# A recurrent attention block on one core: staged operands spread out, value-key products moved to GpSimd, per-array transfer waits, and Ln with Exp for the roots

## The chip, the cores and the metric

The kernel runs on one core of one Trainium2 chip. Its time is device microseconds of one launch; lower is better. Engine names: PE is TensorE, DVE is VectorE, ACT is ScalarE, POOL is GpSimd, SP is SyncE (it only issues transfers here). PSUM is the accumulator memory that PE writes, SBUF the on-chip memory of all engines.

## What is computed

The whole kernel is four pairs of a mixing layer and a feed-forward or expert layer on a tensor `x` of 16 x 256 x 128. The change lies in the first block only, a recurrent attention ("rwkv") with 16 heads of 8 channels and its feed-forward part. Cut to what matters:

```python
def _wkv7(r, w_log, k, v, a, b):
    decay = jnp.exp(-jnp.exp(w_log))
    def step(state, inp):                     # state: batch, head, 8 x 8
        r_t, d_t, k_t, v_t, a_t, b_t = inp
        sa = jnp.einsum('bhij,bhj->bhi', state, a_t)
        state = state * d_t[:, :, None, :] + sa[..., None] * b_t[:, :, None, :] \
                + v_t[..., None] * k_t[:, :, None, :]
        return (state, jnp.einsum('bhij,bhj->bhi', state, r_t))
    ...
kk = kk / jnp.maximum(jnp.linalg.norm(kk, axis=-1, keepdims=True), 1e-12)
o = _wkv7(rh, w_log..., kh, vh, -kk, kk * ah)
o = _gn_heads(o.reshape(Bx, Tx, C), gn_w, gn_b)      # a norm per head, eps 0.00064
x = x + (o + bonus) * g @ W_o
x = x + jnp.square(jax.nn.relu(kf @ W_ffn1)) @ W_ffn2
```

## The kernel before, in words

The block is `rwkv_block` (line 2446). It runs three stages, each a block of its own with a barrier behind it.

**Arrays** (`rwkv_arrays`, line 2481). It loops over 8 pairs of sequences, 512 positions each, in tiles of 128 x 512. PE makes nine products per pair (`items`), with `LENGTHS`, the cross products (`cross`) and the late ones (`late`) between them; ACT takes them out of PSUM (`take`); DVE mixes (`blend`), and does the elementwise work of the pair before (`products`, `across`, `finish`) and of this one (`key`), and the norms of the next (`normalise`, `turn_rows`). `pad` on ACT writes the transposed rows that the next `blend` waits for. Two time steps are folded into one, so the scan has 128 steps. The results sit in the buffers `sent[s]` (r, w, k, v, b), `decay_two[s]` and `keep[s]`, two of each. SP sends them when a pair is finished, with twelve transfers into the scan's layout (five arrays of 2 x 128 KB, decays 2 x 64 KB; line 2547) and one of 768 KB to memory (`kept`, line 2550). ACT, before it takes item `k` of pair i, waits for all of pair i - 2 (lines 2641 and 2642). The lengths of the keys are rooted by ACT (Sqrt, line 2663), clamped and inverted by DVE (lines 2717, 2721). The loops of ACT and DVE are written as loops over pairs of pairs.

**Scan** (`rwkv_scan`, line 2813). 128 steps in 16 blocks of `CK` = 8. The state of a step is 128 partitions x 128 elements (two heads a partition, 8 x 8 each). ACT's `stage(m)` copies a block's operands out of the time-strided arrays (lines 2852 to 2858) into two slots. Per step, DVE multiplies the state in PSUM with the recall and decay vectors (`recalled`, line 2954, two instructions of 192 elements, the vector repeated over i by its access pattern), sums over j (`sa`, line 2960), makes `removed` (line 2964, one instruction of 256 elements for both folded steps), `shown` (line 2974, two instructions of 128) and the next step's value-key products `added` (line 2941). PE adds up the new state in the other PSUM bank: two matmuls with the identity for `added`, one for the decayed state, two for `removed` (lines 2911 to 2917), and in between one eighth of the output sums of the block before (`turn_out`, line 2899).

**Output** (`rwkv_out`, line 2997). Per pair of sequences: the mean and variance per head, the root (Sqrt on ACT, line 3099, reciprocal on DVE, line 3164), the gate, the output product, and the feed-forward part with four hidden tiles. ACT takes the hidden tiles out with Relu (line 3113), POOL squares them (line 3134). ACT does the root of pair i + 1 ahead of `padded` of pair i (`square(i + 1)`, then `ffn.act`), which DVE's `mix` (line 3200) and then PE's hidden matmuls (line 3077) wait for.

Each engine runs its own list in order; semaphores are the only link between them.

## Time and profile before

| what | us |
|---|---|
| median of three runs | 5173.32 (5163.14 to 5174.13) |
| profiled execution, its own time | 5184.22 |
| its span | 5182.1 |
| PE busy in the span | 3937.7 (76%) |
| DVE busy | 2686.7 (52%) |
| ACT busy | 2047.1 (40%) |
| POOL busy | 1004.0 (19%) |

The profile is of one execution. Busy time is that of instructions with work; waits and the issue of transfers don't count. Each part of the block has its own limit, so the shares of the whole span say little about it; the stretches and the timeline do. In a timeline row stand the start, the time, the engine, the line and the operation, output and inputs, and the number of instructions merged.

### The profile page before, as it was taken

The page shows a single profiled execution, that of the slowest core. Times are in us where ns is not written, and L with a number is a line of the kernel's source. Part 1 is how long each engine was busy: PE and PEld are TensorE (multiplying, and loading weights), DVE is VectorE, ACT ScalarE, POOL GpSimd, SP SyncE. Part 2 cuts the span into 40 slices and gives each one's busy share as a digit, 9 for nine tenths or more (in the row PEclk, how much of TensorE's full clock was granted, in tenths as well). Part 3 has the DMA queues.
Part 4 walks back from the last instruction along what each step waited for, and adds up shares of the span by engine and source line. Part 5 has one row for each costly group of instructions (what it writes and reads, how often), then busy time and mean ns, then how long its engine had stood idle before and what let it go on. Part 6 is the DMA issues. An engine that isn't in the chain of part 4 may idle for free. (4 is left out here: it accounts for less than half of the span.)

```text
span 5182.1 us, 64858 instructions
## 1 busy us (share of the span) xinstructions
PE 3937.7 (76%) x19738; PEld 2738.9 (53%) x19800; DVE 2686.7 (52%) x6897; ACT 2047.1 (40%) x4136; POOL 1004.0 (19%) x970
## 2 busy tenths in 40 slices
PE   3548976699976688868886988897899877720498
PEld 1116644377753365646664766675577655520266
DVE  5758967322224676657774344333222255579444
ACT  3322111244433288858883344333333333300132
POOL 1000003100000376546651000000000001144200
PEclk9769987799987699989997999998999966655599
DMA  1440011000000000000000000000000000000000
GB/s 28 64 67 6 4 57 36 37 1 0 0 4 16 17 1 0 1 18 1 0 1 15 1 0 0 0 0 9 25 0 0 5 0 0 0 1 0 17 0 16
DMA packets 45619, 58.53 MB, mean 11 GB/s; under 512 B 14058, under 2 KB 37836, under 8 KB 44588
## 3 DMA queue, kind: packets, MB, share of 16 engines
q1 hardware_dynamic: 45484, 56.92, 4.7%
q8 instruction: 61, 1.00, 0.1%
q14 instruction: 74, 0.61, 0.0%
HBM read 34.87 MB, written 10.51 MB: 9 GB/s over the span
## 5 line engine op out<-in xcount | busy, mean ns | idle before, releaser
L418 PEld LDWEIGHTS bank<-moe_w,moe_hidden 128*128 128x128 f32 x5376 | 626.6, 192 | 78.5 <-issue 76.5
L418 PE MATMUL bank<-moe_w,moe_hidden 128*128 128x128 f32 x5376 | 630.3, 275 | 0.0
L408 PE MATMUL bank<-normed_t,moe_w 128*128 (+1 forms) x1344 | 615.8, 600 | 11.7 <-ACT moe_hidden L470 8.4
L546 DVE SCALAR_TENSOR_TENSOR branch<-bank,moe_weights,branch 128x128 f32<-128x128 f32 x768 | 216.4, 344 | 708.1 <-PE bank L418 704.0
L470 ACT ACTIVATE moe_hidden<-bank,moe_b 128x512 f32<-128x512 f32 x544 | 373.0, 687 | 505.5 <-PE bank L408 504.0
L90 POOL TENSOR_TENSOR branch_norm_shifted<-branch_norm_moments,eps 128x4 f32<-128x4 f32 x64 | 12.8, 200 | 1903.8 <-DVE branch_norm_moments L83 1903.8
L408 PEld LDWEIGHTS bank<-normed_t,moe_w 128*128 128x128 f32 x1344 | 245.0, 193 | 256.6 <-issue 240.4
L1465 DVE TENSOR_TENSOR ssm_mixer<-ssm_decay,bank 128x384 f32<-128x384 f32 x256 | 141.9, 554 | 301.0 <-PE bank L1151 263.3
L1960 POOL TENSOR_TENSOR local_size<-local_size,local_half_powers 128x8 f32<-128x8 f32 x128 | 257.2, 2009 | 201.5 <-DVE local_size L2026 197.5
L1281 ACT ACTIVATE ssm_decay<-bank 128x384 f32<-128x384 f32 x256 | 124.9, 491 | 327.3 <-PE bank L1132 327.2
L1664 PE MATMUL bank<-local_wqkv,local_shifted 128*128 128x512 f32 x384 | 209.5, 637 | 56.0 <-DVEq L2018 24.4
L843 PE MATMUL bank<-ident,attn_scaled 128*128 128x128 f32 x32 | 8.9, 435 | 249.6 <-DVE attn_scaled L808 249.6
L1848 ACT ACTIVATE local_probs<-bank,local_peak 128x128 f32<-128x128 f32 x512 | 182.1, 379 | 8.9 <-issue 8.4
L1067 PE MATMUL bank<-ssm_in_rows,ssm_wbc 128*128 128x512 f32 x256 | 142.6, 676 | 45.1 <-ACTq L1264 44.9
L1164 PE MATMUL bank<-ssm_mixer,ssm_x_wide 128*128 128x256 f32 x512 | 158.9, 392 | 19.4 <-DVE ssm_mixer L1465 19.4
L1150 PE MATMUL bank<-ssm_c_rows,ssm_b_rows 128*128 128x256 f32 x512 | 173.1, 421 | 0.0
L1952 POOL TENSOR_TENSOR local_turned_part<-local_raw,local_tables 128x512 f32<-128x512 f32 x128 | 165.8, 1295 | 28.1 <-ACT local_raw L1827 26.7
L1689 PE MATMUL bank<-local_k_t,local_q_t 128*128 128x128 f32 x1024 | 141.0, 283 | 23.5 <-ACT local_probs L1848 20.7
L1689 PEld LDWEIGHTS bank<-local_k_t,local_q_t 128*128 128x128 f32 x1024 | 140.4, 199 | 27.7 <-issue 20.4
L1965 POOL TENSOR_TENSOR local_probs<-local_probs,local_total 128x512 f32<-128x512 f32 x128 | 133.3, 1041 | 82.9 <-DVE local_total L2050 82.9
L2045 DVE TENSOR_REDUCE local_peak<-bank 128x4 f32<-128x512 f32 x128 | 88.4, 691 | 117.4 <-PE bank L1689 110.4
L843 PEld LDWEIGHTS bank<-ident,attn_scaled 128*128 128x128 f32 x32 | 5.7, 217 | 252.0 <-DVE attn_scaled L808 252.0
(532 smaller groups left out, 8966.8 us busy)
## 6 DMA issues: line engine op xcount, KB each, us to landing
rwkv_kept<-rwkv_keep SPq DMA_DIRECT2D x8, 768.0 KB, 18.5
moe_w<-in_moe_w_dram SPq DMA_DIRECT2D x2, 2304.0 KB
rwkv_gate<-rwkv_kept SPq DMA_DIRECT2D x8, 512.0 KB, 3.4
moe_w<-in_moe_w_dram SPq DMA_DIRECT2D x2, 2048.0 KB
rwkv_recv<-rwkv_sent_r SPq DMA_DIRECT2D x16, 128.0 KB
x<-rwkv_sent_w SPq DMA_DIRECT2D x16, 128.0 KB
rwkv_keys<-rwkv_sent_k SPq DMA_DIRECT2D x16, 128.0 KB
rwkv_values<-rwkv_sent_v SPq DMA_DIRECT2D x16, 128.0 KB
```

Of the source, the lines that this page charges most:

```text
L408: pe.matmul(hbank[n % 4][:], w1[:, e, f * P:(f + 1) * P], source_t[:, bass.ds(i * PN, PN)], start=True, stop=True).then_inc(hidden_up, 1)
L418: last = pe.matmul(obank[e % 2][:, t * P:(t + 1) * P], hid[:, e % 2, f, t * P:(t + 1) * P], w2[:, e, f, :], start=(f == 0), stop=(f == chu ...
L470: act.activation(hid[:, e % 2, f, :], hbank[n % 4][:], ACT.Gelu_apprx_tanh, bias=b1[:, n:n + 1] if bias else 0.0).then_inc(hidden_done, 1)
L546: last = dve.scalar_tensor_tensor(core.branch[:, t, :], obank[e % 2][:, t * P:(t + 1) * P], weights[:, i * PT + t, e - first_routed:e - fi ...
L1067: last = pe.matmul(bank[0:rows, :], wbc[:, n, :], source, start=True, stop=True)
L1150: pe.matmul(gb[:, 0:SEQ], b[:, s[0]:s[0] + P], c[:, s[0]:s[0] + SEQ], start=True, stop=True)
L1164: pe.matmul(ybank[:, c * SEQ:(c + 1) * SEQ], x[0], m[:, 0:SEQ], start=(k == 0), stop=False)
L1664: pe.matmul(bank[:], shifted[:, at, t * P:(t + 1) * P], wqkv[:, part * INNER:(part + 1) * INNER], start=True, stop=True).then_inc(a_up, 1)
L1689: last = pe.matmul(bank[:, w * P:(w + 1) * P], q_t[:, j, c, w, :], keys, start=False, stop=(w == WINDOWS - 1))
L1848: last = act.activation(probs[:, u % 2, w, :], sbank[u % 2][:, w * P:(w + 1) * P], ACT.Exp, bias=peak[:, u % 2, w:w + 1], accum_out=total[ ...
L1952: pool.tensor_tensor(turned_part[:, m % 2, :].rearrange("p (h s d) -> p h s d", s=2, d=HD // 2), rows, sines.broadcast_to([P, HEADS, 2, HD ...
L1960: pool.tensor_tensor(part, part, half_powers[:], ALU.pow).then_inc(scaled, 1)
```

## The change

In the arrays: each array has its own semaphores, and every engine waits for the array that it is about to write. Decays and rates are sent by SP after `products`, `recv` after `finish`, values, recall and keys by ACT (in the queue of ACT). The lengths are clamped by DVE out of PSUM at the end of a pair, and ACT makes the inverse root as exp(-0.5 ln). The loops over pairs of ACT and DVE are written out. In the scan: the staged vectors are written out over i by ACT, so `recalled` and `shown` are one instruction each; `added` is made by POOL; `removed` is made in two instructions with a signal each. In the output part: ACT makes the inverse root with Ln and Exp, and squares the hidden tiles.

```diff
+        def send(queue, n, i, buffer):
+            for j in range(2):
+                b = 2 * i + j
+                queue.dma_start(home[n][b * GROUPS:(b + 1) * GROUPS, :, :],
+                                buffer[:].rearrange("p (j t) -> p j t", j=2)[:, j, :]).then_inc(landed[n][i % 2], 16)
...
-                sp.wait_ge(arrays_ready, i + 1)
-                for array, buffer in zip(arrays, (*sent[s], decay_two[s])):
-                    for j in range(2):
-                        b = 2 * i + j
-                        sp.dma_start(array[b * GROUPS:(b + 1) * GROUPS, :, :],
-                                     buffer[:].rearrange("p (j t) -> p j t", j=2)[:, j, :]).then_inc(arrays_in, 16)
+                sp.wait_ge(rates_ready, i + 1)
+                send(sp, "d", i, decay_two[s])
+                send(sp, "b", i, sent[s][4])
+                sp.wait_ge(recv_ready, i + 1)
+                send(sp, "r", i, sent[s][0])
                 sp.wait_ge(keep_ready, i + 1)
-                sp.dma_start(kept[i], keep[s][:]).then_inc(kept_in, 16)
-            sp.wait_ge(kept_in, 16 * PAIRS)
-            sp.wait_ge(arrays_in, 16 * 12 * PAIRS)
+                sp.dma_start(kept[i], keep[s][:]).then_inc(kept_in[s], 16)
...
                 take("g2", keep[s][:, 1, :], ACT.Identity, g_ready)
-                if has_next:
+                act.wait_ge(values_ready, i + 1)
+                send(act, "v", i, v)
+                if i > 0:
+                    send_keys(i - 1)
+                if i < PAIRS - 1:
                     pad(i + 1)
-                act.wait_ge(lengths_up, i + 1)
-                act.activation(lengths[:], core.bank[LENGTHS][:], ACT.Sqrt).then_inc(lengths_ready, 1)
+                act.wait_ge(lengths_kept, i + 1)
+                act.activation(lengths[:], lengths[:], ACT.Ln)
+                act.drain()
+                act.activation(lengths[:], lengths[:], ACT.Exp, scale=-0.5).then_inc(lengths_ready, 1)
+            def send_keys(q):
+                act.wait_ge(keys_ready, q + 1)
+                send(act, "w", q, sent[q % 2][1])
+                send(act, "k", q, sent[q % 2][2])
...
-                dve.wait_ge(lengths_ready, q + 1)
-                dve.tensor_scalar(lengths[:], lengths[:], 1e-12, None, ALU.max)
                 dve.wait_ge(act_ready, q + 1)
                 dve.tensor_tensor(with_k, k[:], r[:], ALU.mult)
-                dve.drain()
-                dve.reciprocal(lengths[:], lengths[:])
                 dve.tensor_tensor(even(decayed_r), even(d[:]), even(r[:]), ALU.mult)
-                if reused:
-                    dve.wait_ge(arrays_in, (q - 1) * 16 * 12)
+                if q >= 2:
+                    dve.wait_ge(landed["d"][s], 32 * (q // 2))
                 dve.tensor_tensor(decay_two[s][:], even(d[:]), odd(d[:]), ALU.mult)
                 dve.drain()
+                dve.wait_ge(lengths_ready, q + 1)
                 dve.tensor_tensor(w[:], w[:], lengths[:], ALU.mult).then_inc(lengths_used, 1)
...
+            def keep_lengths(i):
+                dve.wait_ge(lengths_up, i + 1)
+                dve.tensor_scalar(lengths[:], core.bank[LENGTHS][:], 1e-24, None, ALU.max).then_inc(lengths_kept, 1)
...
-                    act.wait_ge(shown_ready, m - 1)
+                    act.wait_ge(shown_ready, (m - 1) * CK)
+                    act.wait_ge(added_ready, (m - 1) * CK)
...
-                act.activation(to_sa[:, slot, :, 0:2, :], by_step(recall_w), ACT.Identity)
-                act.activation(to_sa[:, slot, :, 2, :], decays[:, :, m * CK:(m + 1) * CK].rearrange("p x c -> p c x"),
-                               ACT.Identity)
+                def spread(out, array):
+                    for h in range(PH):
+                        act.activation(out[:, :, h * HD * HD:(h + 1) * HD * HD].rearrange("p c (i j) -> p c i j", j=HD),
+                                       array[:, h * HD:(h + 1) * HD, :].rearrange("p j c -> p c j").unsqueeze(2)
+                                       .broadcast_to([P, CK, HD, HD]), ACT.Identity)
+                steps = lambda array, s: array[:, :, at].rearrange("p x (c s) -> p x c s", s=2)[:, :, :, s]
+                for s in range(2):
+                    spread(to_sa[:, slot, :, s, :], steps(recall_w, s))
+                spread(to_sa[:, slot, :, 2, :], decays[:, :, m * CK:(m + 1) * CK])
+                for s in range(2):
+                    spread(to_out[:, slot, :, s, :], steps(recv, s))
                 act.activation(rows_of[:, slot, :, 0:2, :], by_step(rates), ACT.Identity)
                 act.activation(rows_of[:, slot, :, 2:4, :], by_step(keys), ACT.Identity)
-                act.activation(values_of[:, slot], by_step(values), ACT.Identity)
-                act.activation(to_out[:, slot], by_step(recv), ACT.Identity).then_inc(staged, 1)
+                act.activation(values_of[:, slot], by_step(values), ACT.Identity).then_inc(staged, 1)
...
+                    if not (isinstance(c, int) and c == 0):
+                        pe.wait_ge(shown_ready, c)
                     pe.matmul(bank, core.ident[:], added[:, s, 0, :], start=True, stop=False)
                     pe.matmul(bank, core.ident[:], added[:, s, 1, :], start=False, stop=False)
                     pe.wait_ge(recalled_ready, c + 1)
                     pe.matmul(bank, core.ident[:], recalled[:, s, 2, :], start=False, stop=False)
-                    pe.wait_ge(removed_ready, c + 1)
+                    pe.wait_ge(removed_ready, c * 2 + 1)
                     pe.matmul(bank, core.ident[:], removed[:, s, 0, :], start=False, stop=False)
+                    pe.wait_ge(removed_ready, c * 2 + 2)
                     pe.matmul(bank, core.ident[:], removed[:, s, 1, :], start=False, stop=True).then_inc(state_ready, 1)
...
+        @block.gpsimd
+        def _(pool):
+            def add(c, slot, k):
                 out = added[:, k % 2].rearrange("p s (x j) -> p (s x) j", j=HD)
                 v = values_of[:, slot, k].rearrange("p s x -> p (s x)").unsqueeze(2)
                 key = rows_of[:, slot, k, 2:4, :].rearrange("p s (h j) -> p (s h) j", j=HD).unsqueeze(2)
                 shape = [P, 2 * PH, HD, HD]
-                dve.tensor_tensor(out.rearrange("p (a i) j -> p a i j", i=HD),
-                                  v.rearrange("p (a i) o -> p a i o", i=HD).broadcast_to(shape),
-                                  key.broadcast_to(shape), ALU.mult).then_inc(added_ready, 1)
...
-                    for h in range(PH):
...
+                    dve.tensor_tensor(recalled[:, s], state.unsqueeze(1).broadcast_to([P, 3, ST]), to_sa[:, slot, k],
+                                      ALU.mult).then_inc(recalled_ready, 1)
                     dve.drain()
                     dve.tensor_reduce(sa[:].rearrange("p s x -> p (s x)"),
                                       recalled[:, s, 0:2, :].rearrange("p a (x j) -> p (a x) j", j=HD), AX.X, ALU.add)
                     dve.drain()
-                    shape = [P, 2 * PH, HD, HD]
...
+                    shape = [P, PH, HD, HD]
+                    for a in range(2):
+                        dve.tensor_tensor(
+                            removed[:, s, a].rearrange("p (h i j) -> p h i j", h=PH, j=HD),
+                            sa[:, a].rearrange("p (h i) -> p h i", i=HD).unsqueeze(3).broadcast_to(shape),
+                            rows_of[:, slot, k, a, :].rearrange("p (h j) -> p h j", j=HD).unsqueeze(2).broadcast_to(
+                                shape), ALU.mult).then_inc(removed_ready, 1)
                     if k == 0 and not (isinstance(m, int) and m < 2):
                         dve.wait_ge(summed, m - 1)
-                    for h in range(PH):
...
+                    now = dve.tensor_tensor(shown[:, slot, k], state.unsqueeze(1).broadcast_to([P, 2, ST]),
+                                            to_out[:, slot, k], ALU.mult)
+                    now.then_inc(shown_ready, 1)
...
-                act.activation(spread[:], core.bank[0][:], ACT.Sqrt, bias=cols[:, 4:5]).then_inc(rooted, 1)
+                act.activation(spread[:], core.bank[0][:], ACT.Ln, bias=cols[:, 4:5])
+                act.drain()
+                act.activation(spread[:], spread[:], ACT.Exp, scale=-0.5).then_inc(rooted, 1)
...
-                act.wait_ge(hidden_done, i * HC)
+                if has_tail:
+                    act.wait_ge(out_up, i)
                 for f in range(HC):
                     act.wait_ge(hidden_up, i * HC + f + 1)
                     act.activation(relu[:, f, :], core.bank[2 + f][:], ACT.Relu).then_inc(relu_done, 1)
+                    if f > 0:
+                        act.drain()
+                        act.activation(hidden[:, f - 1, :], relu[:, f - 1, :], ACT.Square).then_inc(hidden_done, 1)
+                act.drain()
+                act.activation(hidden[:, HC - 1, :], relu[:, HC - 1, :], ACT.Square).then_inc(hidden_done, 1)
...
-                pool.wait_ge(out_up, i)
-                for f in range(HC):
-                    pool.wait_ge(relu_done, i * HC + f + 1)
-                    pool.tensor_tensor(hidden[:, f, :], relu[:, f, :], relu[:, f, :], ALU.mult).then_inc(hidden_done, 1)
...
-                dve.reciprocal(spread[:], spread[:])
```

## Rows read from the trace of the kernel before

**Rows 1.** Busy time by stretch, the block's stages; stretch, length, engines, PE clock, DMA share, GB/s.
```profile
50.00:366.50 316.50, 155.87 (x272) 53.70 (x272) 225.97 (x513) 109.22 (x143) 19.33 (x32) 0.77 0.35 51
366.50:391.20 24.70, 0.00 (x0) 0.00 (x0) 0.04 (x1) 0.01 (x1) 0.00 (x0) 0.51 0.58 110
391.20:717.00 325.80, 302.67 (x1538) 210.97 (x1538) 281.49 (x897) 54.13 (x112) 0.00 (x0) 0.98 0.02 5
```

**Rows 2.** Busy time by stretch within the arrays; PE, PEld, DVE, ACT, POOL.
```profile
89.08:122.68 33.60, 18.77 (x34) 6.39 (x34) 28.17 (x65) 13.84 (x18) 2.42 (x4) 0.80 0.04 7
122.68:308.95 186.27, 95.70 (x170) 32.80 (x170) 140.83 (x320) 69.19 (x90) 12.08 (x20) 0.73 0.42 60
308.95:366.50 57.55, 27.54 (x40) 9.45 (x40) 38.21 (x67) 14.94 (x19) 0.00 (x0) 0.71 0.48 66
```

**Rows 3.** Waits of the arrays: who waited for whom, total, times, longest.
```profile
ACT rwkv_sent_w L2630 <- DMA rwkv_kept<-rwkv_keep: 75.7, 6, 13.4
```

**Rows 4.** Timeline at the end of a pair of the arrays.
```profile
118.17 0.60 ACT L2631 ACTIVATE rwkv_keep<-bank 128x512 f32<-128x512 f32 x1 [7.27 <-PE bank L2588]
...
120.32 1.26 SPq L2547 DMA_DIRECT2D x<-rwkv_sent_w  x2
...
121.83 0.78 ACT L594 ACTIVATE rwkv_padded<-bank,rwkv_cols 128x512 f32<-128x512 f32 x1 [3.06 <-PE bank L588]
```

**Rows 5.** Groups by line, arrays: busy us, mean ns, idle before.
```profile
L2721 DVE RECIPROCAL rwkv_squares<-rwkv_squares 128x512 f32<-128x512 f32 x8 | 26.8, 3353 | 0.6
```

**Rows 6.** Timeline of one step of the scan.
```profile
501.11 0.62 DVE L2954 TENSOR_TENSOR rwkv_recalled<-bank,rwkv_to_sa 128x192 f32<-128x192 f32 x2
...
502.32 0.43 DVE L2964 TENSOR_TENSOR rwkv_removed<-rwkv_sa,rwkv_rows_of 128x256 f32<-128x256 f32 x1
...
502.80 0.49 PE L2916 MATMUL bank<-rwkv_removed,ident 128*128 128x128 f32 x2
...
503.12 0.39 PE L2917 MATMUL bank<-rwkv_removed,ident 128*128 128x128 f32 x2
...
503.35 1.08 PE L2899 MATMUL bank<-rwkv_shown,ident 128*128 128x256 f32 x2
503.55 0.62 DVE L2954 TENSOR_TENSOR rwkv_recalled<-bank,rwkv_to_sa 128x192 f32<-128x192 f32 x2
...
504.71 0.39 PE L2914 MATMUL bank<-rwkv_recalled,ident 128*128 128x128 f32 x2
```

**Rows 7.** Groups by line, DVE products of other blocks with 384 and 128 elements.
```profile
L1465 DVE TENSOR_TENSOR ssm_mixer<-ssm_decay,bank 128x384 f32<-128x384 f32 x256 | 141.9, 554 | 301.0 <-PE bank L1151 263.3 <-ACT ssm_decay L1281 24.0 <-issue 12.9
...
L2010 DVE TENSOR_TENSOR local_tables<-local_tables,local_scales 128x128 f32<-128x128 f32 x4 | 0.9, 287 | 3.1 <-DMA local_masks<-in_window_dram 3.1
```

**Rows 8.** Groups by line, a POOL product of 256 elements.
```profile
L712 POOL TENSOR_TENSOR attn_products<-attn_qkv 128x256 f32<-128x256 f32 x3 | 2.4, 804 | 1.0 <-DVE attn_scores L753 1.0
```

**Rows 9.** Timeline of the local attention: a PSUM operand on DVE beside POOL.
```profile
2006.80 0.75 DVE L2085 SCALAR_TENSOR_TENSOR local_hidden<-bank,local_cols,local_bent 128x512 f32<-128x512 f32 x1
...
2006.89 1.04 POOL L1965 TENSOR_TENSOR local_probs<-local_probs,local_total 128x512 f32<-128x512 f32 x1 [1.48 <-DVE local_total L2050]
```

**Rows 10.** Timeline of one pair of the output part.
```profile
829.85 0.69 ACT L3099 ACTIVATE rwkv_spread<-bank,rwkv_out_cols 128x512 f32<-128x512 f32 x1 [2.16 <-PE bank L3050]
...
832.85 6.14 PE L3077 MATMUL bank<-rwkv_mix,rwkv_w 128*128 128x512 f32 x8 [3.04 <-DVE rwkv_mix L3200]
...
835.98 1.25 DVE L3166 SCALAR_TENSOR_TENSOR rwkv_centred<-rwkv_centred,rwkv_out_cols,rwkv_gate 128x512 f32<-128x512 f32 x1
...
842.89 1.92 PE L3064 MATMUL bank<-rwkv_wo,rwkv_gated 128*128 128x128 f32 x8
```

**Rows 11.** Groups by line, ACT's strided copies of the scan.
```profile
L2852 ACT ACTIVATE rwkv_to_sa<-x 128x256 f32<-128x256 f32 x16 | 10.1, 633 | 64.5 <-PEq L2487 46.9 <-DVE rwkv_shown L2974 17.5
...
L2853 ACT ACTIVATE rwkv_to_sa<-rwkv_decays 128x128 f32<-128x128 f32 x16 | 6.6, 415 | 0.0
```

**Rows 12.** Timeline of ACT in the wave block: the load ahead of an Exp that follows Ln.
```profile
1542.17 1.28 ACT L2226 ACT_TABLE_LOAD   x1
```

More of the change, by code:

```diff
@@ L2474, in rwkv_block, with rwkv_arrays @@
             decays = ssb("decays", [P, PC, STEPS])
-            rwkv_arrays(core, sem, heads, heads_in, arrays_in, kept_in, kept,
-                        (recv, recall_w, keys, values, rates, decays), GROUPS, HALF, DECAY)
+            rwkv_arrays(core, sem, heads, heads_in, kept, (recv, recall_w, keys, values, rates, decays), GROUPS, HALF,
+                        DECAY)
             rwkv_scan(core, sem, (recv, recall_w, keys, values, rates, decays), mixed_out, out_sent, x_back, x_dram)
         rwkv_out(core, tail, heads, kept, mixed_out, x_back)
-def rwkv_arrays(core, sem, heads, heads_in, arrays_in, kept_in, kept, arrays, GROUPS, HALF, DECAY):
+def rwkv_arrays(core, sem, heads, heads_in, kept, arrays, GROUPS, HALF, DECAY):
     nc, dram = core.nc, core.dram
@@ L2621, in pad, with pair @@
                 act.sem_inc(padded_ready, 1)
-            def pair(i, s, reused=True, has_next=True):
+            def pair(i):
+                s = i % 2
                 r, w, k, v, b = sent[s]
@@ L2940, in add_next, with steps, _ @@
                 shape = [P, 2 * PH, HD, HD]
-                dve.tensor_tensor(out.rearrange("p (a i) j -> p a i j", i=HD),
-                                  v.rearrange("p (a i) o -> p a i o", i=HD).broadcast_to(shape),
-                                  key.broadcast_to(shape), ALU.mult).then_inc(added_ready, 1)
-            def steps(m, slot, last=False):
+                if not (isinstance(c, int) and c < 2):
+                    pool.wait_ge(state_ready, c)
+                pool.tensor_tensor(out.rearrange("p (a i) j -> p a i j", i=HD),
+                                   v.rearrange("p (a i) o -> p a i o", i=HD).broadcast_to(shape),
+                                   key.broadcast_to(shape), ALU.mult).then_inc(added_ready, 1)
+            def steps(m, slot):
+                pool.wait_ge(staged, m + 1)
+                for k in range(CK):
+                    add(m * CK + k, slot, k)
+            steps(0, 0)
+            with pool.Fori(0, BLOCKS // 2 - 1) as h:
+                for slot in range(2):
+                    steps(h * 2 + 1 + slot, 1 - slot)
+            steps(BLOCKS - 1, 1)
+        @block.vector
+        def _(dve):
+            dve.memset(nothing[:], 0.0).then_inc(cleared, 1)
+            def steps(m, slot):
+                dve.wait_ge(staged, m + 1)
                 for k in range(CK):
@@ L2993, in _ @@
             steps(BLOCKS - 2, 0)
-            steps(BLOCKS - 1, 1, last=True)
+            steps(BLOCKS - 1, 1)
 def rwkv_out(core, tail, heads, kept, mixed_out, x_back):
```

119 lines of the change are left out of this document (49 added, 70 removed).

## The prediction

> **What bounds the kernel now.** I first cut the span into its stages with the table of stretches. The diff touches one block of nine, in three stages: the arrays (50 to 366.5 us), the scan (391.2 to 717) and the output part after it. Between the first two stand 24.7 us with no compute at all, while DMA is 58% busy [rows 1]. What follows the block isn't touched and is carried over.
>
> *Arrays.* VectorE (DVE) carries the pair. The pair from 89.08 took 33.60 us with DVE busy 28.17; the next five took 186.27, so 37.25 each, with the same DVE work (140.83 / 5 = 28.17) [rows 2]. The 3.65 us between them are waits, and the list of waits names their origin: ScalarE (ACT) stands 75.7 us in six waits, about 12.6 each, for the transfers of two pairs ago before it can take `k` [rows 3]. That holds up TensorE (PE), and through it DVE.
>
> *Scan.* The timeline shows a loop of dependences. `recalled` starts at 501.11, `removed` at 502.32, PE takes `removed` at 502.80, its second matmul at 503.12, and the next `recalled` starts at 503.55: 1.21 + 0.48 + 0.32 + 0.43 = 2.44 us [rows 6], and 128 of these are 312 of the 325.8 us [rows 1]. PE is nearly full beside it: from the second `removed` matmul (503.12) to `recalled` of the next step (504.71) is 1.59, plus 0.23 for that one (503.12 to 503.35 is the spacing of such a pair) makes 1.82, and 2.05 for the round [rows 6].
>
> **The change part by part.**
>
> *Arrays, middle.* (a) The DVE reciprocal goes, 3.35 us a pair [rows 5], and with it the maximum ahead of it, which moves to the end of the pair, where DVE waits for `padded` anyway; I count 3.6 for both. ACT gets Ln and Exp instead. They run while DVE mixes and does the first products of the next pair, so they cost nothing; if that cover went, it would be two table loads of 1.28 [rows 12] and two activations of about 0.6, 3.8 us a pair. (b) The waits for whole pairs become waits per array, on two queues. Decay and rates go right after `products`, values from ACT right after the g2 item, recall and keys before the next pad. The 12.6 us wait of ACT should go, and with it the 3.65 us on DVE. Bounds: 0 (all transfers as late as now) to 3.65; I take 3.65, because by the new order `w` is issued about 13 us ahead of the need for it (my estimate from the places of g2 and of the wait in the pair), behind four transfers of 128 KB, where now a whole pair's thirteen go out at once. (c) ACT now issues DMAs: six a pair stand between g2 and pad. SyncE pays 1.26 for two, so six cost 3.8 us. g2 starts at 118.17 and ends at about 118.8; pad could start at 122.6 instead of 121.83 [rows 4], so 0.8 to 0.9 later, and DVE's next mix waits for pad. Bounds 0 and 3.8. For pair 0 there are two sends: about +1.2. Sum: pair 0 +1.2; pair 1 -3.6 + 0.9 = -2.7; the five others -(3.6 + 3.65 - 0.9) = -6.35 each, -31.8.
>
> *Arrays, end.* The last stretch, 308.95 to 366.5, has DVE busy only 38.2 of 57.6 [rows 2]. ACT's wait there goes too (12.8 of it), but the last lengths now pass through six sends (3.8), a load, Ln, a load, Exp (3.8) before DVE may go on: I estimate -9, bounds -2 and -13. After it the 24.7 us: now the last pair's twelve sends and the 768 KB of `kept` all begin at its end. Afterwards only two sends of `recv` and `kept` begin there, with `w` and `k` 6 us earlier on their own queue. That leaves about half of the traffic: -11, bounds -4 and -17. Arrays together: 1.2 - 2.7 - 31.8 - 9 - 11 = -53.
>
> *Scan, the loop.* `recalled` becomes one instruction of 384 elements. The same kind with one operand in PSUM takes 554 ns [rows 7], now two take 0.62: -0.07. `removed` becomes two of 128 elements; such a one takes 287 ns [rows 7] against 0.43: the first matmul starts 0.14 earlier. The second half ends 0.2 later, and PE comes to it 0.32 after the first, so it isn't late. 2.44 - 0.21 = 2.23 a step; DVE itself needs less than 2 without `added`. 128 x 0.21 = -27; I take -26. Bounds: none, if PE's three more waits a step cost 0.2 us; -50, if the step falls to PE's 2.05.
>
> *Scan, GpSimd (POOL).* A product of 256 elements on POOL takes 804 ns in the attention block [rows 8]. It starts when the state of two steps ago is out, at the same moment as `recalled`, and is needed some 3 us later: hidden, twofold. Its price if it isn't lies in a rival.
>
> What it may disturb is DVE. The trace has both sides: a DVE instruction with one operand in PSUM took its usual 0.75 while POOL multiplied [rows 9], one with its tensors all in SBUF took 1.25 beside POOL [rows 10]. `recalled` and `shown` are of the first kind. `removed` is of the second, but starts 1.14 us after the state, when POOL's 0.80 are over. So zero.
>
> The Trainium skill ("SBUF — State Buffer", section "Who interferes with whom") says that a VectorE instruction with two SBUF inputs and a GpSimd one that reads SBUF exclude each other for the whole instruction. By that rule, the trace agrees for the SBUF case (1.25 against 0.75) and for the PSUM case; its own result is the third rival.
>
> *Scan, staging.* ACT now writes ten spread pieces of 512 elements instead of three smaller copies. The strided copies cost 415 ns for 128 elements and 633 for 256 [rows 11], 1.7 ns an element; 512 give 1.07, about 0.97 from start to start. Ten and the three others make 11.3 us a block against 3.1. Per block of eight steps (17.8 us) it fits and hides; at the start nothing hides it: +8. Bounds: +3 (if broadcast reads are as cheap as 256 elements now) and +12. Scan: -26 + 8 = -18.
>
> *Output part.* The reciprocal leaves DVE, the squares leave POOL (and DVE's 1.25 goes back to 0.75 [rows 9, 10]). But on ACT, Ln (0.69) is followed by a load of 1.28 and an Exp of 0.63 ahead of `padded`: Exp after Ln is loaded anew in the wave block [rows 12]. So `padded` and `mix` come 2.0 us later. The hidden matmuls start at 834.9 instead of 832.85, take 6.14, and with 0.7 for the transposes the next ones can start at 841.7 instead of 842.89 [rows 10]: -1 a pair, -7. Bounds: +2 a pair (+14) if ACT's squares hold PE, -3.4 a pair (-24).
>
> The skill's "ScalarE: Activation LUTs" (section "Table sets") says that one set holds both functions and Ln then Exp needs one load. The row of the wave block shows a load before each, so I go by the row; by the rule `padded` would be 1.3 us earlier and the part some 9 us shorter.
>
> **The sum.** -53 - 18 - 7 = -78. The profiled run took 5184.2, so 5106 for it. It stands 10.9 over the median of the three shown runs, 5173.3; against that median the forecast is 5095.
>
> **Rivals.**
>
> 1. *ACT as a DMA queue is in the way.* A send to a full queue stands still, and on ACT it holds pad and so DVE; and `w` may land late. For: six issues are 3.8 us of an in-order engine, and it is already 0.9 late by my sum. Against: at most six are outstanding. Price: 4 us a pair over seven pairs, 28. Total -50, 5123.
>
> 2. *PE is the bound of the scan.* For: 2.05 of 2.44 are matmuls, and three waits are added. Then the step stays near 2.4 and the scan gains 4 and loses 8 at the start. Total -53 + 4 - 7 = -56, 5117.
>
> 3. *The other side: POOL holds `removed`.* If POOL's product runs later than I think (it waits for its slot, or takes over 1.1 us), each step's two `removed` wait for it, up to its whole 0.80. The step is then 3.03, the scan +76 + 8, the total 84 - 53 - 7 = +24, 5197. It decides from 0.6 us a step on (the other terms give 52 us, or 0.41 a step, on top of the 0.21). For: all tensors of `removed` are in SBUF. Against: 0.34 us of distance.
>
> 4. *The staging on ACT doesn't fit a block.* It would take 1.55 us a piece; at 2 us a block is 22.0 against 8 x 2.44 = 19.5 now, and the scan +40: total -20, 5153.
>
> **How the numbers follow.** Forecast 0.60, rival 1 0.18, rival 2 0.11, rival 3 0.06, rival 4 0.03, and 0.02 for no change. A measurement of this kernel can tell about 0.2%, 10 us, from no change. Faster 0.89, same 0.04, slower 0.07. Low end: -53 - 11 more from the end of the arrays and the start, -26, -16 in the output part and the staging at +3, near 5060. High end: rivals 1 and 2 together with half of the bound in the output part, 5145.
>
> **What would show it.** Right: pairs of about 31 us in the arrays with no ACT wait of 12 us; a gap before the scan of 13 to 15 us; steps of 2.23; POOL near 0.8 busy per step and `removed` near 0.29; first `recalled` 11 us after the first staging piece; output pairs of 26. Wrong: `removed` above 0.4 (rival 3), PE without idle time in a step (2), pad waiting on ACT's own queue (1). The prediction falls if the transfers on two queues land no earlier than on one.

## The result, and the profile after

The changed kernel took 5095.72 us (median of four runs, 5086.59 to 5100.58) beside 5173.73 for the kernel before in the same comparison; the ratio is 0.9851, with a 95% interval of 0.9831 to 0.9871. The forecast was 5095. The time fits better than the parts do, so the parts are what is worth reading. The profiled execution took 5086.59 (span 5084.6) beside 5184.22: 97.6 less, against 78.0 between the medians; the forecast for it was 5106.

The milestones of both traces, in us:

| stretch | before | after | change | forecast |
|---|---|---|---|---|
| arrays, pair 0 (from 69.28 / 69.12) | 19.80 | 21.45 | +1.65 | +1.2 |
| arrays, pair 1 | 33.60 | 30.10 | -3.5 | -2.7 |
| arrays, five pairs | 186.27 | 152.91 | -33.4 | -31.8 |
| arrays, last stretch (to 366.5 / 320.5) | 57.55 | 46.92 | -10.6 | -9 |
| no compute, up to the scan | 24.7 | 10.4 | -14.3 | -11 |
| scan, start to first `recalled` | 3.1 | 11.0 | +7.9 | +8 |
| scan, first to last `recalled` | 311.4 | 285.9 | -25.5 | -26 |
| output, up to the first `delta` | 49.3 | 51.6 | +2.3 | 0 |
| output, seven pairs | 180.7 | 163.2 | -17.5 | -7 |
| output, last pair and up to the router | 41.7 | 41.8 | +0.1 | 0 |
| router of the first expert layer | 17.3 | 28.9 | +11.6 | 0 |
| all behind it | 4187.1 | 4171.0 | -16.1 | 0 |

These rows of stretches of the changed kernel answer to [rows 1, 2] and have their columns.

```profile
320.50:330.90 10.40, 0.00 (x0) 0.00 (x0) 0.00 (x0) 0.00 (x0) 0.00 (x0) 0.50 0.51 126
330.90:631.00 300.10, 285.51 (x1522) 206.07 (x1523) 231.40 (x641) 189.74 (x222) 80.28 (x128) 0.97 0.02 6
90.57:120.67 30.10, 18.60 (x34) 6.31 (x34) 25.20 (x64) 14.50 (x19) 2.41 (x4) 0.80 0.24 37
120.67:273.58 152.91, 89.81 (x170) 29.96 (x170) 125.65 (x316) 72.51 (x95) 12.07 (x20) 0.81 0.45 74
273.58:320.50 46.92, 23.96 (x40) 8.22 (x40) 31.49 (x64) 17.54 (x22) 0.00 (x0) 0.75 0.50 86
```

A pair of the arrays is 30.58 now (152.91 / 5), with DVE busy 25.13; before it was 37.25 with 28.17 busy. So 3.0 us of the 6.7 are work that left DVE, and 3.6 are waits that went. The transfers are spread over the whole pair (DMA 24% busy already in the second pair, where it was 4%), and ACT's wait of 12.6 us [rows 3] is gone. The end of one pair, from the timeline (start, length, engine, line, operation):

```profile
173.93 0.60 ACT L2644 ACTIVATE rwkv_keep<-bank 128x512 f32<-128x512 f32 x1 [3.23 <-PE bank L2600]
...
174.64 1.29 ACTq L2541 DMA_DIRECT2D rwkv_values<-rwkv_sent_v  x2
...
175.97 1.28 ACTq L2541 DMA_DIRECT2D x<-rwkv_sent_w  x2
...
177.28 2.07 ACTq L2541 DMA_DIRECT2D rwkv_keys<-rwkv_sent_k  x2
...
179.46 0.78 ACT L594 ACTIVATE rwkv_padded<-bank,rwkv_cols 128x512 f32<-128x512 f32 x1 [4.93 <-PE bank L588]
180.30 0.69 DVE L2731 TENSOR_TENSOR rwkv_delta<-rwkv_padded 128x512 f32<-128x512 f32 x1 [1.12 <-ACTq L2632]
```

ACT's six sends fill it from 174.64 to 179.35, and `pad` comes only then, DVE's `delta` behind it: this is what answers to [rows 4]. The six were costed at 3.8 us and take 4.2 to 5.3 in the seven pairs that have six: the last two (keys) take 1.5 to 2.6 instead of 1.26. The trace before has the same at the end of a pair, where the last two of twelve sends took 1.9 to 4.5.

One step of the scan, which answers to [rows 6]:

```profile
500.33 0.56 DVE L3010 TENSOR_TENSOR rwkv_recalled<-bank,rwkv_to_sa 128x384 f32<-128x384 f32 x1 [0.27 <-PE bank L2959]
500.37 0.63 POOL L2984 TENSOR_TENSOR rwkv_added<-rwkv_values_of,rwkv_rows_of 128x256 f32<-128x256 f32 x1 [1.61 <-PE bank L2959]
...
501.47 0.49 DVE L3018 TENSOR_TENSOR rwkv_removed<-rwkv_sa,rwkv_rows_of 128x128 f32<-128x128 f32 x2
501.49 0.39 PE L2955 MATMUL bank<-rwkv_recalled,ident 128*128 128x128 f32 x2
...
501.82 0.49 PE L2957 MATMUL bank<-rwkv_removed,ident 128*128 128x128 f32 x2
...
502.14 0.39 PE L2959 MATMUL bank<-rwkv_removed,ident 128*128 128x128 f32 x2
...
502.57 0.56 DVE L3010 TENSOR_TENSOR rwkv_recalled<-bank,rwkv_to_sa 128x384 f32<-128x384 f32 x1 [0.27 <-PE bank L2959]
```

1.14 + 0.35 + 0.32 + 0.43 = 2.24; the forecast was 2.23. POOL's product takes 0.63 and is over (501.00) 0.47 us before `removed` starts. Ahead of the steps stands the staging on ACT, thirteen pieces from 330.91 on, and the first `recalled` at 342.17.

One pair of the output part, which answers to [rows 10]:

```profile
769.50 1.28 ACT L3140 ACT_TABLE_LOAD   x1
...
770.80 0.69 ACT L3140 ACTIVATE rwkv_spread<-bank,rwkv_out_cols 128x512 f32<-128x512 f32 x1
...
771.54 1.28 ACT L3142 ACT_TABLE_LOAD   x1
...
772.83 0.63 ACT L3142 ACTIVATE rwkv_spread<-rwkv_spread 128x512 f32<-128x512 f32 x1
773.37 0.76 ACT L594 ACTIVATE rwkv_padded<-bank,rwkv_out_cols 128x512 f32<-128x512 f32 x1
774.20 0.69 DVE L3239 TENSOR_TENSOR rwkv_delta<-rwkv_padded 128x512 f32<-128x512 f32 x1 [1.93 <-ACTq L3150]
...
775.77 6.19 PE L3118 MATMUL bank<-rwkv_mix,rwkv_w 128*128 128x512 f32 x8 [5.11 <-DVE rwkv_mix L3243]
...
777.94 1.11 DVE L99 TENSOR_SCALAR fresh<-x,x_norm_moments,x_norm_rstd 128x128 f32 x4
...
781.79 0.60 PE L171 MATMUL bank<-ident,fresh 128*128 128x128 f32 x4
782.23 1.06 PE L3105 MATMUL bank<-rwkv_wo,rwkv_gated 128*128 128x128 f32 x8
```

A load stands before Ln and another before Exp, as forecast. From `mix` (774.96) to the next wo matmuls is 7.27 us; it was 10.85 (832.04 to 842.89, [rows 10]). DVE is done with `fresh` at 779.05, and PE comes to it only at 781.79, when the hidden matmuls (those of L3118) are through: PE sets that half of the pair now.

The router of the first expert layer, which the diff doesn't touch, before (first fence) and after (second), as rows of stretches (the first with PE alone, the second with all engines):

```profile
977.70:995.04 17.34, 16.93 (x81) 0.89 0.00 0
```

```profile
884.70:913.60 28.90, 28.50 (x81) 15.79 (x82) 1.79 (x16) 5.42 (x8) 0.00 (x0) 0.50 0.00 0
```

The same 81 matmuls ran at a mean granted clock of 0.89 before (0.50 for the first 3.5 us, then 1.00) and at 0.50, the lower level, throughout the 28.9 us after.

### The profile page after: what moved, and what is told of

Read it like the earlier page. It is cut to its first block and busy times, and to the rows that moved or that the text cites. A ratio compares the mean times of both kernels' runs of the same rounds, so it can differ in the third digit from the quotient of the medians.

```text
span 5084.6 us, 65295 instructions
## 1 busy us (share of the span) xinstructions
PE 3893.2 (77%) x19738; PEld 2713.3 (53%) x19800; DVE 2569.9 (51%) x6625; ACT 2231.9 (44%) x4312; POOL 1045.3 (21%) x1066
## 5 line engine op out<-in xcount | busy, mean ns | idle before, releaser
L470 ACT ACTIVATE moe_hidden<-bank 128x512 f32<-128x512 f32 x128 | 76.5, 597 | 152.1 <-PE bank L408 152.1
## 6 DMA issues: line engine op xcount, KB each, us to landing
rwkv_kept<-rwkv_keep SPq DMA_DIRECT2D x8, 768.0 KB, 15.2
```

What stands on the lines that cost most here:

```text
L470: act.activation(hid[:, e % 2, f, :], hbank[n % 4][:], ACT.Gelu_apprx_tanh, bias=b1[:, n:n + 1] if bias else 0.0).then_inc(hidden_done, 1)
```

## The experiments

The verdicts rest on stretches, each read from one trace, and not on the whole time, in which single runs of one kernel lie up to 0.5% apart. Where the code of a stretch is the same, it repeats: steps of the scan within 0.4% (2.246 to 2.254), pairs of the arrays 29.19 to 29.67 (nine traces), pairs of the output part 23.31 to 23.59 (nine). For the pairs and steps I give rows of tiles: least, middle and largest length in ns, and the first and last start; from these a pair is (last - first) / 7 and a step (last - first) / 127. The changed kernel's own rows are these (a pair of the arrays, a step, a pair of the output part), and the fourth is the output part before:

```profile
L2731 DVE TENSOR_TENSOR rwkv_delta<-rwkv_padded x8: 691/692/693, 69.1 to 273.6; 128x512 f32<-128x512 f32 x8
L3010 DVE TENSOR_TENSOR rwkv_recalled<-bank,rwkv_to_sa x128: 557/558/559, 342.2 to 628.1; 128x384 f32<-128x384 f32 x128
L3239 DVE TENSOR_TENSOR rwkv_delta<-rwkv_padded x8: 692/692/730, 679.7 to 842.9; 128x512 f32<-128x512 f32 x8
L3196 DVE TENSOR_TENSOR rwkv_delta<-rwkv_padded x8: 692/693/728, 755.3 to 936.0; 128x512 f32<-128x512 f32 x8
```

### The scan

**The products back on VectorE.**

```diff
-                pool.tensor_tensor(out...).then_inc(added_ready, 1)      # GpSimd
+                dve.tensor_tensor(out...).then_inc(added_ready, 1)       # VectorE, behind shown
```

> The changed kernel with one part undone: the value-key products go back from GpSimd to VectorE, behind `shown`. Two bounds theory (before, VectorE's own order and the loop of dependences both took 2.44 us, so each part of the scan's change pays only together with the other): VectorE's order is 0.65 + 0.49 + 0.41 + 0.34 + 0.48 = 2.37 us from start to start, the step is 2.37 in place of 2.24, and the scan is 16 us longer than in the changed kernel, the block too. Loop only (as the prediction told it): the step stays 2.24 and the time is the changed kernel's within noise.

```profile
L2993 DVE TENSOR_TENSOR rwkv_recalled<-bank,rwkv_to_sa x128: 552/558/559, 344.2 to 629.9; 128x384 f32<-128x384 f32 x128
```

The step is 2.25, as with GpSimd; the kernel took 5096.58 (a single run). My own favourite, two equal bounds with 2.37, falls. It had taken 0.48 for `added` from a step in which part of that was waiting; without a wait it is 0.35:

```profile
501.38 0.42 DVE L3008 TENSOR_TENSOR rwkv_shown<-bank,rwkv_to_out 128x256 f32<-128x256 f32 x1
...
501.71 0.41 DVE L2983 TENSOR_TENSOR rwkv_added<-rwkv_values_of,rwkv_rows_of 128x256 f32<-128x256 f32 x1
...
502.06 0.56 DVE L2993 TENSOR_TENSOR rwkv_recalled<-bank,rwkv_to_sa 128x384 f32<-128x384 f32 x1
```

VectorE is without a gap here, and the loop of dependences is just as long (2.24). The move to GpSimd earns nothing; it only leaves VectorE 0.27 us a step.

**Only that move.** Vectors staged compact, `recalled` and `shown` in two instructions, `removed` in one.

```diff
-                    dve.tensor_tensor(recalled[:, s], state..., to_sa[:, slot, k], ALU.mult)
+                    for h in range(PH):   # two of 192, vector repeated by its access pattern
+                        ...
```

> The changed kernel, but of the scan's changes only the move of the value-key products to GpSimd is kept: the vectors are staged compact again, `recalled` and `shown` are two instructions each, `removed` is one. Two bounds or loop only: the loop of dependences is that of before, so the step is 2.44 us, and VectorE stands idle some 0.4 us of it, waiting for TensorE; the scan loses 25 us in its steps against the changed kernel and gets 8 back at its start. Rival (before, the order on VectorE alone was the bound, and the loop had room): the step falls to 2.2 or below.

**`removed` in one instruction.**

```diff
-                    for a in range(2):
-                        dve.tensor_tensor(removed[:, s, a]..., ALU.mult).then_inc(removed_ready, 1)
+                    dve.tensor_tensor(removed[:, s]..., ALU.mult).then_inc(removed_ready, 1)
```

> The changed kernel with `removed` again in one instruction of 256 elements. Loop of dependences: TensorE's first matmul on it starts 0.14 us later, so the step is 2.38 in place of 2.24 and the scan 17 us longer. Rival (the second half or TensorE sets the step, so the split brings nothing): the step stays within 0.03 of 2.24.

The two in this order:

```profile
L3004 DVE TENSOR_TENSOR rwkv_recalled<-bank,rwkv_to_sa x256: 345/353/359, 336.1 to 648.0; 128x192 f32<-128x192 f32 x128
```

```profile
L3009 DVE TENSOR_TENSOR rwkv_recalled<-bank,rwkv_to_sa x128: 557/558/559, 346.6 to 649.6; 128x384 f32<-128x384 f32 x128
```

Steps of 2.456 (before: 2.452) and 2.386. The split of `removed` is worth 0.135 a step, 17 us. The other 0.07 is `recalled` in one instruction; `shown` was changed with it, but VectorE stands idle 0.4 us ahead of the next `recalled` in the first of the two, so its length doesn't count there. The kernels took 5111.27 and 5109.85 (single runs).

**The first block staged by three engines.**

```diff
+                if m == 0:          # ScalarE: four pieces of to_sa, VectorE: six, GpSimd: rows and values
+                    spread(to_sa[:, slot, :, 0, :], steps(recall_w, 0))
+                    spread(to_sa[:, slot, :, 2, :], decays[:, :, 0:CK])
```

> The changed kernel, but the first block of the scan is staged by three engines: ScalarE writes four of the ten spread pieces, VectorE (idle there) six, GpSimd the three small ones. If the start of the scan costs what ScalarE's thirteen pieces take (11.3 us), the first `recalled` comes about 5 us after the first piece instead of 11.3, and the kernel is 6 us faster. Rival: VectorE's copies in the spread pattern are slow beside GpSimd's (both all in SBUF), and the start stays at 8 us or more.

The first `recalled` came 4.9 us after the start of the scan instead of 11.0; the median of four was 5088.26, ratio 0.9825 (0.9808 to 0.9841).

```profile
332.59 2.23 DVE L3043 COPY rwkv_to_sa<-x 128x512 f32<-128x512 f32 x2
...
334.74 2.67 DVE L3043 COPY rwkv_to_out<-rwkv_recv 128x512 f32<-128x512 f32 x4
...
337.59 0.56 DVE L3022 TENSOR_TENSOR rwkv_recalled<-bank,rwkv_to_sa 128x384 f32<-128x384 f32 x1 [0.17 <-issue]
```

### The output part

**Squares back on GpSimd**, Ln and Exp kept:

```diff
-                        act.activation(hidden[:, f - 1, :], relu[:, f - 1, :], ACT.Square)...
+                    pool.tensor_tensor(hidden[:, f, :], relu[:, f, :], relu[:, f, :], ALU.mult)...
```

> The changed kernel with the squares of the hidden tiles back on GpSimd (Ln and Exp stay). The output part took 23.3 us a pair against 25.8 before. Theory A (VectorE's stretch from `mix` to `fresh` held TensorE before, mostly by the reciprocal): GpSimd's squares slow VectorE's all-SBUF instructions again by 0.6 to 1.5 each, about 3 us, which the end of the hidden matmuls hides almost wholly (fresh ends 2.5 us before them now): 23.3 to 24.3 a pair. Theory B (the squares beside VectorE were the main cost): 25 or more a pair.

**Reciprocal back on VectorE**, squares kept on ScalarE:

```diff
-                act.activation(..., ACT.Ln, bias=cols[:, 4:5]); act.activation(..., ACT.Exp, scale=-0.5)
+                act.activation(..., ACT.Sqrt, bias=cols[:, 4:5])        # and dve.reciprocal(spread, spread)
```

> The changed kernel with the root of the output part made as before, Sqrt on ScalarE and reciprocal on VectorE; squares stay on ScalarE. Theory A: `padded` comes 2.0 us earlier, VectorE's stretch after `mix` grows by 3.3, so `fresh` is ready 0.8 us after the hidden matmuls end; 2.0 earlier plus 0.8 to 1.0 later gives about 22.3 a pair, 1 us less than the changed kernel. Theory B (Ln and Exp are the gain of the part): 24 or more a pair.

**`padded` ahead of Ln and Exp:**

```diff
                 act.sem_inc(padded_ready, 1)
+                if has_next:
+                    root(i + 1)         # Ln and Exp, taken out of square(i + 1)
```

> The changed kernel, but ScalarE writes `padded` of a pair ahead of Ln and Exp for the next pair's root. If the load and the Exp ahead of `padded` hold `mix` by 2.0 us as the prediction said, then VectorE's own work (ready at 772.3 where `delta` now starts at 774.2) is next, and a pair is 1.9 us shorter, the part 13 us. Rival: the gate then waits for the root, and `fresh` and the wo matmuls come as much later: no change.

The three in this order:

```profile
L3238 DVE TENSOR_TENSOR rwkv_delta<-rwkv_padded x8: 691/692/729, 684.6 to 849.0; 128x512 f32<-128x512 f32 x8
```

```profile
L3238 DVE TENSOR_TENSOR rwkv_delta<-rwkv_padded x8: 691/694/729, 678.3 to 831.4; 128x512 f32<-128x512 f32 x8
```

```profile
L3244 DVE TENSOR_TENSOR rwkv_delta<-rwkv_padded x8: 692/728/730, 677.8 to 827.8; 128x512 f32<-128x512 f32 x8
```

With before and after this gives us per pair:

| | squares on GpSimd | squares on ScalarE |
|---|---|---|
| Sqrt, reciprocal on VectorE | 25.81 | 21.87 |
| Ln and Exp on ScalarE | 23.49 | 23.31 to 23.59 |
| Ln and Exp behind `padded` | not run | 21.43 |

The table isn't a sum. From before, either edit alone takes VectorE off the stretch between `mix` and `fresh`: 3.9 for the squares alone, 2.3 for the root alone. With the squares on ScalarE, VectorE's all-SBUF instructions no longer run beside GpSimd, and its way from `mix` to the end of `fresh` is 7.1 us instead of 9.9; the rest of the 3.9 goes with a higher granted clock over the seven pairs (0.81 against 0.72) and wasn't taken apart. Both together give no more than the root alone: once PE sets that stretch, Ln, Exp and the second load in front of `padded` cost 1.4 to 1.7 more than the removed reciprocal gives. As the trace of the squares back on GpSimd shows, `fresh` takes 1.83 beside GpSimd instead of 1.11, and nobody waits for it:

```profile
760.64 1.83 DVE L99 TENSOR_SCALAR fresh<-x,x_norm_moments,x_norm_rstd 128x128 f32 x4
...
764.35 0.60 PE L171 MATMUL bank<-ident,fresh 128*128 128x128 f32 x4
```

The order with `padded` first took 5075.90 (four runs, 5065.81 to 5090.31), ratio 0.9804 (0.9781 to 0.9827); its part is 18.4 us shorter than in the changed kernel, 13.2 in the pairs and 5.2 ahead of them. The first two were single runs, 5085.97 and 5070.47, so whole times don't rank the three; the pairs do.

### The arrays

**All sends on SyncE:**

```diff
-                act.wait_ge(values_ready, i + 1)
-                send(act, "v", i, v)
-                    send_keys(i - 1)
+                sp.wait_ge(values_ready, i + 1); send(sp, "v", i, sent[s][3])
+                sp.wait_ge(keys_ready, i + 1); send(sp, "w", i, sent[s][1]); send(sp, "k", i, sent[s][2])
```

> The changed kernel with all sends on SyncE's queue (values, recall and keys too, each after its own signal). If ScalarE's six issues a pair cost what the prediction says (0.9 us a pair, 1.2 for pair 0) and the waits per array are what frees ScalarE, the pairs are 0.5 to 1 us shorter than now (30.6 a pair): 29.8. Rival (the second queue is what makes the transfers land in time): ScalarE waits for `w` again, and the pairs go towards 33.

**The wait for the whole pair back:**

```diff
-                free("w")
+                free("w", "k", "v", "b", "r", "d")
+                act.wait_ge(kept_in[s], 16 * (i // 2))
```

> The changed kernel, but ScalarE waits before item k for every array and the kept rows of two pairs ago, as before; queues and the moments of the sends stay. If the early sends alone suffice, nothing moves (30.6 a pair). If it is the wait per array that counts, ScalarE stands some us before `k` again, VectorE with it, and a pair is 1 to 3.65 us longer.

**The reciprocal back:**

```diff
-                act.activation(lengths[:], lengths[:], ACT.Ln); act.activation(..., ACT.Exp, scale=-0.5)
+                act.activation(lengths[:], lengths[:], ACT.Sqrt)        # and dve.reciprocal in products
```

> The changed kernel with the inverse lengths made by Sqrt on ScalarE and the reciprocal on VectorE again. By the prediction VectorE carries the pair, so each of six pairs is 3.35 us longer, some 20 us in all, and the last stretch 3.35 minus what ScalarE saves of Ln, load and Exp there (about 1.9). Rival (TensorE or ScalarE carries the pair now): less than 1 us a pair.

In this order:

```profile
L2726 DVE TENSOR_TENSOR rwkv_delta<-rwkv_padded x8: 692/692/693, 68.7 to 267.5; 128x512 f32<-128x512 f32 x8
```

```profile
L2733 DVE TENSOR_TENSOR rwkv_delta<-rwkv_padded x8: 691/692/694, 68.9 to 274.4; 128x512 f32<-128x512 f32 x8
```

```profile
L2729 DVE TENSOR_TENSOR rwkv_delta<-rwkv_padded x8: 691/693/694, 68.7 to 305.9; 128x512 f32<-128x512 f32 x8
```

28.40, 29.36 and 33.89 us a pair, over seven pairs, beside 29.21 in the changed kernel's own trace.

One queue is 0.81 a pair better (0.79 against the lowest of the nine traces), and the scan starts 8.5 us earlier (322.7). So the sends on ACT cost what was forecast for them, and the second queue buys nothing: the transfers land in time from one. ACT waits for no transfer in either trace, and the 768 KB of `kept` landed 9.6 us after their issue (median) instead of 15.2. The Trainium skill ("Trainium Kernel Development and Optimization", section "Key Constraints") says that DMAs of all queues share the same DMA engines, so that issuing from several saves only issue time; the trace agrees, with 28.40 against 29.21. The single run took 5095.66 in spite of the 8.5. Its router took 29.0 us, as in the changed kernel's profile (28.9), but all behind it took 4187.4 against 4171.0.

With the whole pair waited for, ACT does stand, but it has that time to spare; five waits of 3.3, where before there were six of 12.6:

```profile
ACT rwkv_sent_w L2643 <- DMA rwkv_keys<-rwkv_sent_k: 16.4, 5, 4.3
```

Yet the pair is where it was (29.36, inside the scatter): with the sends early, a wait for each array buys nothing. That it is the early sends that count follows from these two experiments by exclusion. Early sends weren't undone alone, one queue and the whole-pair wait weren't run together, and the loops written out were never undone. (5101.60, a single run.)

The reciprocal costs 4.68 a pair, more than its 3.35 of work. The rest is again ACT's queue: `pad` waits behind sends that, as I read it, start later because g2 does. DVE waits 29.5 us for it in eight waits, where the changed kernel has 17.2 (the first of the eight is 2.3 in both), and 6 x 3.35 + 12.3 = 32.4 of the 32.7 us by which the seven pairs grew. (5129.95, a single run.)

```profile
DVE rwkv_delta L2729 <- ACTq L2632: 29.5, 8, 5.3
```

### The clock ahead of the router

```diff
+            if name == "moe0":
+                for _ in range(12):
+                    pe.matmul(hbank[0][:], core.ident[:], source_t[:, 0:PN], start=True, stop=True)
             pe.wait_ge(weights_in, 16 * loads)
```

> The changed kernel with twelve matmuls of 512 columns (results thrown away) on TensorE while it waits for the weights of the first expert layer. In the changed kernel the router of that layer ran its whole 28.8 us at TensorE's lower clock, in the kernel before only the first 3.5 us, which cost 10.8 us. If the clock follows what TensorE did just before, the router runs at the higher clock and the kernel is 10 to 14 us faster in the profile than the changed one. Rival: the clock's turns there are a matter of when the stretch falls, and the router stays low or is high by chance; then the time is the changed kernel's within 0.2%, or 5 us more if the added matmuls run late.

```profile
871.20 12.21 PE L376 MATMUL bank<-normed_t,ident 128*128 128x512 f32 x24 [2.01 <-PEq L64]
886.22 1.88 PE L383 MATMUL bank<-normed_t,moe_router 128*8 x4 [2.81 <-DMA moe_router_b<-in_moe_router_b_dram]
```

The router took 15.6 us, at a granted clock of 1.00. In the twelve traces without these matmuls it took 17.0 to 29.4 (17.0, 17.3, 21.0, 21.0, 21.0, 21.1, 24.3, 24.3, 28.9, 29.0, 29.0, 29.4), always after an idle gap of some 17 us in PE. The kernel took 5086.54 (median of five), ratio 0.9828 (0.9814 to 0.9843), beside 0.9851 (0.9831 to 0.9871) of the changed kernel: 12 us by the ratios and 9 between the medians, with intervals that still overlap. What the twelve matmuls do to the router is shown twice (here and in the next kernel); that they shorten the whole kernel is not clear of the noise.

### All four in one

> Four pieces in one kernel: all sends of the arrays on SyncE's queue, the scan's first block staged by three engines, `padded` of the output part ahead of Ln and Exp, and the twelve matmuls ahead of the first router. If the stretches are independent, their gains add: 8.5 in the arrays, 6.1 at the scan's start, 18.4 in the output part (13 in its pairs, 5 ahead of them), and a router of 15.6 us where 17 to 29 were seen. Against the changed kernel's median of 5095.7 that is 33 us for the first three and some 8 for the router: 5055, a ratio to the kernel before of 0.977. Rival: the shorter stretches get a lower granted clock, or the transfers on one queue run into the scan, and less than 30 us remain.

5053.26 us (five runs, 5043.16 to 5062.07), ratio 0.9760 (0.9743 to 0.9776): 42 us below the changed kernel, and 124 below the kernel before in the same comparison (5177.46). In the trace the last `recalled` starts 15.2 earlier than in the changed kernel and the last `delta` of the output part 33.4 (forecast 33.0), and the router took 16.0. The stretches are independent, and their gains add up to there. Behind the router the profile has 4184.1, against 4171.0.

## Why the prediction was right, and where its terms were off

**Arrays, forecast -53, measured -60.** The three sums over pairs came within 2 us each. Right in mechanism: VectorE carried the pair, and what was taken off it showed. How much of the 3.6 us of waits that went is due to the transfers isn't shown, since PE's granted clock in these pairs rose too (0.73 to 0.81, PE busy 95.7 to 89.8 us over five pairs). The cost of the sends (0.9 forecast) is 0.81. The reciprocal was costed at 3.6 a pair, and undoing it costs 4.68, 32.7 us over seven pairs. Too small were the two estimates at the end, -9 and -11 against -10.6 and -14.3 (the gap before the scan is 10.4, not 13 to 15). One reason that I gave didn't hold: of "per array, on two queues", neither half is needed while the other stays. I had written that the prediction falls if two queues land the transfers no earlier than one; all on one queue did as well, so by my own sign that part has fallen, and the sum was right without it because the sends are early.

**Scan, forecast -18, measured -17.6.** Each term within 0.5 us: staging piece 1.07 forecast and 1.09 measured, `recalled` 0.558, `removed` 0.288, step 2.24. The start cost 7.9 against 8. GpSimd's product took 0.63, not 0.80, and `removed` never met it. It was costed at nothing, and the experiment gives nothing. But my remark that VectorE needs less than 2 us without it hid that with it the order needs 2.24, exactly the loop's length: had the loop been shorter by any further edit, the move would begin to pay. That is worked out from the two orders (2.24 with the product, 1.97 without) and wasn't run.

**Output part, forecast -7, measured -15.2.** Here the term was mis-sized: "-1 a pair" was -2.5, and in place of pairs of 26 there are pairs of 23.3. The delay of `mix` by 2.0 us was right, as the run with `padded` first shows (1.9 a pair back). From `mix` to the wo matmuls I had 3.2 less, and it is 3.6 in the pair shown. The larger miss is on the way back, from the wo matmuls to the next `mix`: it took 16.34 before (842.89 to 859.23), I added the 2.0, and it takes 16.45 (758.51 to 774.96). What paid for the delay is PE at a higher granted clock: the 32 matmuls of the output tiles took 5.38 and take 3.83 (clock 0.68 and 1.00), the variance product 2.08 and 1.12 (0.50 and 1.00). Against them stands 0.5 us by which the 32 begin later, since PE waits 1.2 us for ACT's last square. Over the seven pairs, before and after, PE's busy time and its clock (eighth number) are:

```profile
755.00:936.00 181.00, 113.56 (x412) 71.18 (x412) 135.20 (x324) 33.28 (x54) 60.68 (x69) 0.72 0.11 32
```

```profile
680.00:843.00 163.00, 95.78 (x412) 57.79 (x412) 94.53 (x317) 68.02 (x99) 26.11 (x41) 0.81 0.12 36
```

The same 412 matmuls were busy 17.8 us less. The step that failed is that I took over PE's lengths at the old clock. Why the clock is higher there isn't shown. Its mean over the stretch is no measure either: with the squares back on GpSimd it is 0.72 again, and the pair is still 23.49, for the 32 matmuls take 3.83 in every pair there too. The +2.3 ahead of the first `delta` I had left out: from the first `normed` to it 9.2 us became 12.1. Of these 2.9, 2.0 are the load and the Exp ahead of `padded`, which have nothing beside them there, and 0.9 is the second pair's variance product, which ran at a clock of 0.50 where it had 1.00 before (2.08 us for 1.13). 1.1 came back from the first pair's missing reciprocal.

**What was in no term.** The router took 11.6 us more, and all behind it 16.1 less than in the profiled execution before. These runs don't show that either is the change's doing: the router varies by 12 us over the twelve traces without added matmuls, and the rest by 17 (4171.0 to 4187.9) over all fourteen. Up to the router the block became 93.0 us shorter in the two profiles; the medians differ by 78.0, with an interval of 67 to 87. So the spread between executions is hardly the whole of the 15 us between, though single stretches behind the block vary by as much. What remains open is whether the changed kernel meets the slow router more often than the kernel before, since each kernel has one trace. So the hit at 5095 is partly luck: the sum gave the block 15 us too little, and 15 of what the block gained are missing between the medians, for a reason that no run shows. For the profiled execution the forecast, 5106, was 19 too high.

**The ends of the range.** They were added up wrongly, without effect here: the terms named for the low end make -103, so 5070 and not 5060, and those for the high end give 5145 before anything is added for the output part.

**Rivals.** ACT's queue is in the way, and its sign is there (`pad` behind the sends), but by 0.8 a pair, which the sum already had, not 4. PE isn't the bound of the scan, though only just: between the matmuls at 501.49, 501.82 and 502.14 it stands 0.1 us each time, so it needs 2.04 of 2.24. GpSimd doesn't hold `removed`. The staging fits its block: ACT is busy 11.9 of 18.0 us (189.74 / 16).

## What to carry to other kernels

Cost an edit on the stretch that waits last, and then ask what the next edit still finds there: in the output part either of two edits took VectorE off the path, and the second cost more than it gave. Send as early as the data is ready, from an engine that does nothing else; here that did the work, and a wait per buffer added nothing to it. Where matmuls stand behind an idle gap, price them at both clock levels, and read a whole-kernel difference below 0.3% stage by stage, since an untouched stage can give or take more than the edit.

## What the runs showed of the hardware

The same 81 small matmuls after the same idle gap took from 17.0 to 29.4 us, because the granted clock rose from 0.50 to 1.00 after 2.7 to 3.5, after 11 or after 18 us, or not at all in 28.5 us of busy time (four of the twelve traces); twelve matmuls of 512 columns in the gap made it 15.6 and 16.0, both times they were there. A product of 256 elements on GpSimd took 0.63 us in the scan and 0.80 in the attention block [rows 8]. VectorE's `recalled`, with one operand in PSUM, took 0.558 with GpSimd's product beside it and 0.558 without; its spread copies of 512 elements, all in SBUF, took 1.06 to 1.19 beside GpSimd's copies and 0.58 to 0.67 alone. Two sends of 128 KB take their engine 1.26 to 1.3 us; the last two of twelve in a row (64 KB each) took 1.9 to 4.5, and 1.26 where nothing had been sent in the 5 us before.
